# Pairs of rows through a conditioned residual chain: channels on partitions for gates and soma, x read turned, context average in PSUM, fused norms

## What is computed

```python
x = x + x @ W0[subject].T + b0[subject]                                   # layer 0
h = relu(x @ W1[lang] + b1[lang])                                         # layer 1
x = x + layernorm(x + h @ W2[lang] + b2[lang]) * gamma[lang] + beta[lang]
ctx = causal_ema(x)                                                       # layer 2
g   = x * sigmoid([x, ctx] @ Wg.T + bg)
mod = 0.5 + sigmoid(gelu(x @ Wn1.T + bn1) @ Wn2.T + bn2)                   # 32 modulations
temporal = sum_d blend[d] * causal_ema_d(g * mod[d])                      # 32 decays
out = (gelu(x @ Wsoma.T + bsoma) * sigmoid(temporal @ Wtemp.T + btemp)) @ Wout.T
x = x + layernorm(out) * gamma2 + beta2
x = x + zX*lap_x(x) + zY*lap_y(x) + zR*x*(1-x)                            # layer 3
```

## Time and profile before

| what | value |
|---|---|
| median of three runs | 1193.43 us (1192.27 to 1195.39) |
| profiled execution, first to last instruction | 1192.3 us |
| PE, PEld busy | 90%, 70% |
| DVE, POOL, ACT busy | 65%, 56%, 36% |
| mean granted TensorE clock | 0.983 of full speed |
| moved by DMA | 90.39 MB, 76 GB/s |

### The profile page before, as it was taken

How to read it: one execution, slowest core, us unless ns; L and a number is a source line. 1 busy time by engine, 2 the same in 40 slices (tenths; PEclk the granted TensorE clock), 3 DMA queues, 4 the chain that set the end, 5 groups by cost and what they waited for, 6 DMA issues and landing times.

```text
span 1192.3 us, 19407 instructions
## 1 busy us (share of the span) xinstructions
PE 1078.3 (90%) x5802; PEld 831.6 (70%) x5896; DVE 779.8 (65%) x1247; ACT 430.7 (36%) x778; POOL 671.9 (56%) x974
## 2 busy tenths in 40 slices
PE   0259999999999999999999999999999999999994
PEld 0137777777777777777778777777787777777772
DVE  6645666676676666666766667667666766666662
ACT  4242333333333334433333343334333433333331
POOL 5544555556665555566655555665555556655553
PEclk9968999999999999999999999999999999999998
DMA  5422222222212222222122222222222222222100
GB/s 175 132 62 65 78 77 84 71 79 85 73 62 88 70 88 70 79 74 85 62 88 70 80 78 79 70 82 68 83 75 79 71 87 70 73 77 78 37 10 18
DMA packets 61670, 90.39 MB, mean 76 GB/s; under 512 B 5124, under 2 KB 22063, under 8 KB 61652
## 3 DMA queue, kind: packets, MB, share of 16 engines
q1 hardware_dynamic: 61236, 89.49, 24.9%
q0 software_dynamic: 352, 0.63, 0.3%
q10 hardware_dynamic: 64, 0.05, 0.0%
HBM read 81.76 MB, written 8.39 MB: 76 GB/s over the span
## 4 chain that ended last, share of the span: by engine, by line
PE 70%; DVE 15%; POOL 5%; issue 4%; ACT 3%; DMA 2%; DVEq 1%; SPq 0%; POOLq 0%; ACTq 0%
PE bank L971 28%; PE bank L978 13%; PE bank L958 8%; PE bank L1016 7%; DVE work L924 4%; PE bank L1143 3%; PE bank L1045 3%; PE bank L964 3%; PE bank L1162 2%; DVE work L918 2%; ACT work L651 2%; DVE work L894 2%; POOL work L422 2%; DVE work L777 2%; DMA work<-in_L_cond_Wg 1%
## 5 line engine op out<-in xcount | busy, mean ns | idle before, releaser
L461 POOL TENSOR_TENSOR temph<-work,temph 128x512 fp32r<-128x512 f32 x32 | 41.4, 1295 | 349.9 <-ACT temph L618 349.9
L813 DVE TENSOR_TENSOR work<-bank,work 128x512 f32<-128x512 f32 (+7 forms) x256 | 108.3, 454 | 120.4 <-PE bank L1016 111.4
L411 POOL TENSOR_TENSOR work<-work 128x448 f32<-128x448 f32 (+6 forms) x224 | 163.5, 730 | 31.0 <-DVE work L813 20.5
L958 PE MATMUL bank<-ident,work 128*128 128x128 f32 x768 | 122.4, 282 | 46.4 <-DVE work L924 35.4
L1016 PEld LDWEIGHTS bank<-ms,vj 128*128 128x128 f32 x1024 | 139.1, 191 | 26.7 <-issue 15.4
L958 PEld LDWEIGHTS bank<-ident,work 128*128 128x128 f32 x768 | 85.1, 141 | 85.0 <-DVE work L924 50.2
L1016 PE MATMUL bank<-ms,vj 128*128 128x128 f32 (+7 forms) x1024 | 140.1, 272 | 0.0
L1029 PE MATMUL bank<-temph,amath 128*128 128x512 f32 x384 | 102.0, 401 | 0.0
L839 DVE SCALAR_TENSOR_TENSOR work<-work 128x512 f32<-128x512 f32 x32 | 22.1, 692 | 117.6 <-ACT work L569 117.6
L791 DVE TENSOR_TENSOR work<-bank,blend_n 128x512 f32<-128x512 f32 x128 | 84.2, 676 | 22.4 <-PE bank L1029 22.4
L971 PE MATMUL bank<-w_r,temph 128*128 128x512 f32 x256 | 92.3, 443 | 2.4 <-DVE w_r L765 2.4
(11 more groups left out here) (193 smaller groups left out, 2418.7 us busy)
## 6 DMA issues: line engine op xcount, KB each, us to landing
w_land<-in_L_cond_weight SPq DMA_DIRECT2D x64, 512.0 KB, 3.7
w_t<-in_L_cond_W SPq DMA_DIRECT2D x64, 256.0 KB, 2.7
work<-in_x SPq DMA_DIRECT2D x32, 256.0 KB, 2.6
gamma_t<-in_L_cond_gamma SPq DMA_DIRECT2D x32, 256.0 KB, 3.1
work<-in_L_cond_beta SPq DMA_DIRECT2D x32, 256.0 KB, 3.3
out<-work SPq DMA_DIRECT2D x32, 256.0 KB, 4.1
work<-in_L_cond_Wg SPq DMA_DIRECT2D x2, 1024.0 KB, 9.2
work<-in_L_cond_Wsoma SPq DMA_DIRECT2D x1, 1024.0 KB, 9.5
```

Of the source, the lines that this page charges most:

```text
L411: g_.tensor_tensor(dst, dst, src, ALU.add).then_inc(S["acc_ready"], 1)
L813: ins = v_.tensor_tensor(pj[:, slot, cols].rearrange("p (a t) -> p a t", a=CC), ring[(w + 1) % 2][:, cols].rearrange("p (a t) -> p a t", a ...
L958: ins = nc.tensor.transpose(dst[:, a * P:(a + 1) * P], src[:, a * P:(a + 1) * P], ident[:, :])
```

## The change

Two rows now form a pair, and a step handles three pairs (16 pairs, 14 steps with all three). By part:

- The products with Wg (both halves), Wsoma, Wtemp and Wn1 are made with the weight block stationary and the activations of both rows moving (256 columns); each output block of 128 channels lies on partitions in a bank of its own. Biases enter as per-partition columns in the activation that reads the bank. Layer 0, layer 1's second product and Wout keep time on partitions, a row at a time.
- x comes a second time from HBM, already turned by the host (`xT`); soma and gate leave the matmul turned, so x and sg are turned no more; nor are h and h1.
- The context average is a scan within PSUM: Wg's second half is applied to x2, DVE scans the product in its bank, and Wg's first half is added onto it.
- The chunk products have 256 - 32*j columns for a pair. `chunk_terms` and `add_terms` go in ten halves (two channel blocks of both rows) in place of five tiles a row, with two slots of `prod`.
- The norms take the mean and gamma in one pass of DVE and rstd with the addition in a second; `rstd` on POOL is two instructions, and the two normalising passes of ACT are gone.
- Constants are prepared inside the first steps; low parts of all five matrices are made by DVE.

```diff
-            def split(dst, lhs, rhs, first=0, blocks=range(CC), stop=False):
-                split_hi(dst, lhs, rhs, first, blocks)
-                return split_lo(dst, lhs, rhs, first, blocks, stop)
+            def cols_times(dst, weight, act, first_block, o, onto=False):
+                for a in range(CC):
+                    for w_part, x_part in ((0, 0), (0, 1), (1, 0)):
+                        ins = mm(dst, weight[:, w_part, first_block + a, o * P:(o + 1) * P], act[:, x_part, a],
+                                 start=(not onto and a + w_part + x_part == 0), stop=(a == CC - 1 and w_part == 1),
+                                 skip_group_check=onto)
...
+            def ctx_sums(p, a):
+                dve.wait_ge(S["z2_done"], CC * p + a + 1)
+                v_.tensor_tensor_scan(GATES[a][:, 0:W2], ctx_decay[:, :, :].rearrange("p r t -> p (r t)"), GATES[a][:, 0:W2], 0.0,
+                                      ALU.mult, ALU.add).then_inc(S["z2_summed"], 1)
...
+            def chunk_weights(p, n):
+                if n == 0:
+                    pe.wait_ge(S["ms_ready"], p + 1)
+                if n < 2:
+                    pe.wait_ge(S["soma_ready"], CC * p + n + 1)
+                else:
+                    pe.wait_ge(S["p_ready"], NT * p + n - 1)
...
+            def chunk_terms(p, n):
+                dve.wait_ge(S["w_done"], NT * p + n + 1)
...
+                if n >= 4:
+                    dve.wait_ge(S["acc_ready"], N_ADD * p + ADDS[n - 1])
...
+            def state(p, r, s_):
+                b = 2 * p + r
+                if s_ == 0:
+                    pe.wait_ge(S["amatlo_ready"], b + 1)
+                    pe.wait_ge(S["glo_ready"], b + 1)
+                    if r == 0:
+                        pe.wait_ge(S["p_ready"], NT * p + NT - 1)
...
+            def centred(p, r):
...
+                v_.scalar_tensor_tensor(xs[:, r], xs[:, r], mv_a[:, 0:1], gamma_t[:, :], ALU.subtract, ALU.mult).then_inc(S["t1_ready"], 1)
+            def x2_row(p, r):
...
+                v_.scalar_tensor_tensor(xs[:, r], xs[:, r], rs_a[:, 1:2], xb, ALU.mult, ALU.add).then_inc(S["x2_ready"], 1)
```

More of the change, by code:

```diff
@@ L237, in first, with live, past, second @@
+        S = {n: sem(n) for n in names}
+        def live(p):
+            return not isinstance(p, int) or 0 <= p < NP
+        def past(p, n):
+            return not isinstance(p, int) or p >= n
         def first(i):
             return isinstance(i, int) and i == -2
+        def second(i):
+            return isinstance(i, int) and i == -1
         def steps(engine, step):
@@ new lines, in step @@
+                    temporal(Cr, 1)
+                    temporal_lo(Cr, 1)
+                if live(A):
+                    y_row(A, 0)
+                    y_stats(A, 0)
+                    w0_lo(A, 1, 1)
+                if first(i):
+                    lo_parts(0)
+                    vj_parts(range(2, Q))
+                if live(A):
+                    y_aggregate()
+                if live(Cr):
+                    soma_gate(Cr, 0)
+                if live(A):
+                    centred(A, 0)
@@ L900, in step @@
-                if live(B):
-                    chunk_terms(B, NW - 1)
-                if live(A):
-                    aggregate(st_a, mv_a, 1)
-                if live(B):
-                    for s_ in range(NG - 2):
-                        states_blend(B, s_)
-                if first(i):
-                    lo_parts(4)
+                if live(A + 1):
+                    w0_lo(A + 1, 0, 1)
+                if live(B):
+                    chunk_terms(B, 2)
+                if live(A):
+                    y_row(A, 1)
+                    y_stats(A, 1)
@@ L953, in _, with turn, rows_times @@
             mm = nc.tensor.matmul
-            def turn(dst, src, n=CC):
-                for a in range(n):
+            def turn(dst, src):
+                for a in range(CC):
                     ins = nc.tensor.transpose(dst[:, a * P:(a + 1) * P], src[:, a * P:(a + 1) * P], ident[:, :])
                 return ins
-            def whole(dst, lhs, rhs, blocks=range(CC), start=False):
+            def rows_times(dst, act, weight, blocks, start, stop):
                 for a in blocks:
-                    ins = mm(dst, lhs[:, a * P:(a + 1) * P], rhs[:, a], start=(start and a == 0), stop=(a == CC - 1))
-                return ins
@@ L1033, in soma_part, with blend_rows @@
[L1033 to L1047 removed]
+            def blend_rows():
+                pe.wait_ge(blend_soft, KG)
+                for a in range(CC):
+                    ins = nc.tensor.transpose(bank[7][:, a * P:(a + 1) * P], bl_rep[:, a].rearrange("p r d -> p (r d)"), ident[:, :])
+                ins.then_inc(blend_back, 1)
```

1748 lines of the change are left out of this document (1020 added, 728 removed).

## The result

The changed kernel takes **1267.57 us** (median of 4 runs, 1264.58 to 1268.12) against 1192.85 before: a ratio of 1.062, 95% interval 1.059 to 1.064. The prediction said 1268.0 and slower. Its profiled execution spans 1266.3 us.

The account below looks back on a forecast made before the run. TensorE's own list was taken as the limit. A pair step was 60.9 + 8.4 + 2.2 + 1.0 + 1.5 = 74.0 us against 68.4; 136 + 1036 + 56 + 39 = 1267, forecast 1268 us, range 1150 to 1340.

Parts of the forecast that it names:

- TensorE's work: TensorE's list for a pair of rows: work falls from 66.4 to 60.9 us.
- idle in the tail: Between the second row's adapter and the first row's states, PE idles 8.4 us of 13.5, waiting for DVE and POOL.
- second row's states: Before the second row's states, whose weights are built after the first row's states: PE idles 2.2 us a pair.
- elsewhere: Other PE waits in a step (h's ReLU behind t_hi on ACT, x1's turn): 1.0 us.
- low clock: Granted clock may fall in the waiting stretch: 1.5 us a pair added, bounds 0 and 5.1 (a whole episode every step).
- The price of 256 columns: Each of 204 TensorE instructions of 256 columns costs 0.134 us, 27.3 us a pair, floor 0.12 and ceiling 0.163.
- a clock under 1.00 in most steps: Granted clock of TensorE under 1.00 in most steps, listed as a sign that the prediction is wrong.
- The ends: Outside the fourteen full steps: 136 us ahead (bounds 120 to 150), 56 and 39 us behind.
- The chain hides: Wait between adapter(A,1) and state(0,0) stays covered; not slower, 1100 to 1185 us, break-even 68.6 a pair; chance 0.20.
- The narrow price is better still: The 204 products of 256 columns cost 0.108 each, a pair 68.7, the whole 1193 us, no change; chance 0.08.
- more is lost: Price 0.163 (1350 us), a full clock episode each step (1318), or DVE passes held up beside POOL (1309); chance 0.22.
- expected gain of 5.5 us a pair: TensorE's shorter list would gain 5.5 us a pair, plus saved idle time, if nothing else moved.

Follow-up runs that it names:

- e12: Changed kernel with 8, 4 and 11 unused 512-column matmuls ahead of the three waits and 6 ahead of the second row's states: 1265.34 us.
- e7: Kernel before, with only Wsoma's product issued as 24 instructions of 256 columns instead of 12 of 512: 1193.53 us, ratio 0.9995.
- e1: Changed kernel, with POOL's x2_plus_beta of the second row moved behind its last chunk addition: 1260.53 us.
- e2: Changed kernel, with DVE's chunk_terms(3) ahead of y and its statistics, the aggregate after term 4, POOL's add_terms(3) ahead of rstd: 1255.68 us.
- e5: Changed kernel with the edits of e1 and e2, and on DVE g's low part and term 6 ahead of x2_row, `final` behind term 7: 1241.86 us.
- e6: e5 with the second row's state weights made between chunk_terms(8) and chunk_terms(9) in DVE's list: 1216.6 us.
- e10: Changed kernel with only the second row's state weights moved up between chunk_terms(8) and chunk_terms(9) in DVE's list: 1254.6 us.
- e9: e6 with two of soma's four parts moved behind the adapter and the low part of the next W0 behind g's: 1194.0 us.
- e11: e8 with layer 2's norm also changed to two DVE passes, in place of one ACT pass and two POOL passes: 1153.86 us.
- e3: Changed kernel with 5, 3 and 6 unused 512-column matmuls put ahead of the three waits between adapter and states: 1284.9 us.
- e4: Changed kernel with layer 0 of the next pair's first row moved from the step's head into the waiting stretch before: 1272.19 us.
- e8: Kernel before, with only layer 1's norm in the changed form (two fused DVE passes, shorter rstd, no ACT normalising pass): 1177.62 us.

## Why the prediction was right

The time, the sign and the place came out; the kernel is TensorE's list with one uncovered chain in it. By the prediction's steps, for the pair step of 72.0 us (74.0 predicted):

| term | predicted | measured |
|---|---|---|
| TensorE's work | 60.9 | 58.3 (72.0 less the four below) |
| idle in the tail | 8.4 | 6.2 (2.09, 1.21, 2.91) |
| second row's states | 2.2 | 2.6 (0.78, 1.79) |
| elsewhere | 1.0 | 1.8 (0.34, 0.85, 0.63) |
| low clock | 1.5 | 3.1 at most (states 4.78 against 3.03, turn of x2 1.09 against 0.46, four chunk products 1.15 against 0.47) |

The turn is that from 640.84 to 641.93 against the one at 653.22 in the same step, the chunk products those at 639.69 against the four at 632.08; a short wait may hide in the last figure, as e12 has one of 0.23 there. The 74.0 is 2.0 too long by errors of -2.6, -2.2, +0.4, +0.8 and +1.6, in the table's order: the sum is closer than its terms.

- **The price of 256 columns** was mis-sized: (669.55 - 663.84)/48 = 0.119 us, not 0.134, and so below the lower bound of 0.12 by a hair. I took the value between two estimates with an overhead for each instruction; e7 shows that there is none. For 204 instructions that is 3.1 us a pair. The work came out 2.6 lower, so the other items of PE's list cost 0.5 more than I counted; which ones I did not separate. The Trainium skill (TensorE: Matmul & The Clock Gate, Back-to-back issue gap) gives 262 cycles, an estimate of 0.109; the trace shows 10% more.
- **The tail** has nearly the predicted length (13.8 to the end of the last term, 13.5 predicted) for partly other reasons. I let POOL bind from rstd on. POOL's additions are slower than I took them (1.90 for a pair in place of 1.58), but its x2_plus_beta costs nothing, since DVE's x2, `final` and g stand ahead of term 6. e1 shows this (no wait moved), e2 and e5 show the layers: order first, DVE's list next, POOL's additions last, at 10.9 us. PE idles for 2.2 less than predicted: the first row's states start at 641.93, 1.6 before the last term ends, chunk products and turn are stretched by the low clock, and matmuls ahead of a wait run to modelled ends, which count as work. How the 2.2 divide was not measured.
- **The clock** falls in the waiting stretch as the earlier trace rows suggested, in every full step. It costs up to 3.1 us of matmul time, twice the 1.5 in the sum and inside its bounds of 0 and 5.1; by e12 it gives back only 0.8 a step when it is restored, as the chunk terms bind next. The prediction also listed a clock under 1.00 in most steps as a sign that it was wrong. That sign came true, and it contradicts the prediction's own term for the clock.
- **The second wait** is there, 1.79 long. That removing it shortens the step is shown on e5 (by e6), not on after: in e10 the 1.4 us taken from it came back in the first row's states.
- **The ends** were 19 too short. The product with Wn1 starts 4.5 us into a step (658.15 - 653.68); in the first full step it starts at 152.45, fourteen steps on at 1168.46. So 148 us stand ahead, not 136, 102 behind, not 95, and the fourteen take 1016, not 1036 (72.6 on average). So the 1268 is so close by luck: errors of +20 and -19 cancel; each by itself would have left the forecast within 2%. At the start PE waits 12.25 us at 84.68 for x2's turn; the splits of the large weights stand in ACT's and DVE's lists between the pieces of the first pair's norm (timeline of after, all engines):

```profile
78.69 2.19 ACT L548 ACTIVATE wtemp_r<-work 128x512 fp32r<-128x512 f32 x4 [3.56 <-DVE wsoma_r L806]
79.35 2.50 DVE L806 SCALAR_TENSOR_TENSOR wtemp_r<-work,wtemp_r 128x512 fp32r<-128x512 f32 x4 [1.11 <-ACT wtemp_r L548]
...
84.68 1.08 PE L1213 MATMUL bank<-ident,work 128*128 128x128 f32 x4 [12.25 <-ACT work L589]
```

- **The other signs.** PE is busy for 80% of the span (85 forecast), POOL has no idle time from rstd to the last addition, and the other engines come out as counted: DVE 50, ACT 22 and POOL 31 us a pair (625, 278 and 387 us in 900). `xT` costs nothing: no wait of PE in the step is for a transfer.
- **The rivals.** "The chain hides" did not come about, but e9 shows how near it was: three reorderings bring the pair to 68.0 us, under the 68.6 that I gave as its break-even, and the time to that of before. "The narrow price is better still" was half right (0.119, not 0.108). Of "more is lost" the low clock came, not as a whole episode, and L1059 was held up by 0.5 us, and each of three pairs of POOL's additions by 0.3.

What the expected gain of 5.5 us a pair met is then this: a shorter list, but a list in which the long products no longer lie over the chain from the adapter through DVE and POOL to the states. The edits to the tail, one on top of the other, give 1267.6 (after), 1260.5 (e1), 1241.9 (e5), 1216.6 (e6), 1194.0 (e9). The part of the change that pays without pairing, the fused norms, gives 1153.9 (e11). Open: whether the paired order with its clock restored would come under e11; it was not tried.

## What to carry to other kernels

Count a new schedule by what lies on top of each cross-engine chain, not by the sum of the limiting engine: a list whose work is 8 us shorter (58.3 against 66.4) lost 4 us a step when its fillers moved ahead of the chain. A wait that is removed pays less than its length as long as the next list in the chain is close behind (DVE's order, DVE's list, POOL's additions in turn), and can pay more where it also moves a low clock off the work behind it (e6, 2.1 for 1.4), so write the chain once for each engine before pricing an edit. Read an edit's worth from the ordinary step, not from the total: in e10 the total fell by 13 us and the ordinary step by 0.2. When a rewrite bundles several edits, try the smallest one on the old kernel first: here it alone beat both kernels.

## What was not expected of the hardware

- **Waits that the profile puts on nothing.** In 2 of the 14 steps of after, at 729.50 and 878.29, PE stands still before layer 0 for 3.84 and 2.78 us with the reason "issue": the profile names nothing that it waits for. These steps take 77.4 and 74.9 us instead of 72. e12 has four, 146 us apart, of 2.6 to 2.9, and each such step is 4 us longer, 1.5 of it by the clock: the window 728 to 736 above has 0.79, and twelve matmuls take 4.61 where those at 653.68 of after take 3.11. That eats what e12 won. The kernel before and e11 have no such gap over 1 us in their steady stretch. The queue of instruction loads moved 0.15 MB in the kernel before and 0.70 in after, and in after and in e12 each gap lies beside loads on it (in e12, 0.03 MB between 727 and 733), while the steps of after at 436 and 580, without such loads, have no gap on PE. Of the edits, e1, e6 and e10 have one such gap each (2.9, 3.8 and 3.9 us), e9 two, e3 and e4 have shorter ones too, and e5, without such loads beside a step's head, has none; but e2 has the loads (0.05 MB between 424 and 438) and a gap of only 0.6. That the loads cause it was not tested. For the comparisons above it means that up to 8 us of a difference can come from the number of these steps.
- **The clock falls without one long pause.** In after the pauses ahead of the fall are 2.09, 1.21 and 2.91 us with narrow products between them. Adding work can move the fall instead of lifting it (e3, five steps of fourteen), or lift it (e12, seven of fourteen).
- **Contention shows on both sides.** A DVE pass with two SBUF inputs took 1667 ns beside POOL's addition (e8) and 752 without it (e11, and the first two rows of e8). In after L1059 takes 1.24 us beside POOL's additions and 0.75 where POOL is idle (613.67), and a pair of these additions takes 1.90 against 1.58.
